# Keys turned by the vector engine from a second, split read, in a cross-attention, attention and expert kernel

## Reference

```
x (8,64,512), ctx (8,1601,512)
x = x + softmax((LN(x) Wq + bq)(ctx Wk + bk)^T / sqrt(512)) (ctx Wv + bv)   # cross-attention, 1 head
x = x + gated_attention(LN(x))    # 16 heads of 32; sigmoid((cos(q,k) - 0.295) * 15) with gates, then Wo
x = x + experts(LN(x))            # 8 experts, top 1, sigmoid of the best logit, SiLU-gated, 512 -> 256 -> 512
```

## Time and profile before

| | us |
|---|---|
| runs: median (lowest to highest) of 3 | 393.93 (393.82 to 394.73) |
| profiled execution: span, first to last instruction | 391.0 |
| TensorE busy in it | 363.3 |
| VectorE, ScalarE, GpSimd busy in it | 147.2, 93.3, 82.2 |
| bytes moved, mean rate | 56.48 MB, 144 GB/s |

### The profile page before, as it was taken

One profiled execution on the slowest core, in us unless ns is written; L12 is line 12 of the kernel. 1 busy time (PEld: TensorE's weight loads), 2 busy tenths in 40 slices (PEclk: granted clock), 3 DMA queues, 4 the chain that ended last, 5 costly groups with the idle time before them and its releaser, 6 DMA issues.

```text
span 391.0 us, 6077 instructions
## 1 busy us (share of the span) xinstructions
PE 363.3 (93%) x2346; PEld 232.2 (59%) x2346; DVE 147.2 (38%) x341; ACT 93.3 (24%) x191; POOL 82.2 (21%) x87
## 2 busy tenths in 40 slices
PE   1999999999999999999999999999889989799993
PEld 1786667435646544565654455653435869697781
DVE  4100365003616523351652444342362654155322
ACT  2222321213215331222541222241302400000000
POOL 4000243500215002022400201202322402511122
PEclk9999998999999999999999999999999999899998
DMA  7999200399700029710004950000693052920000
GB/s 256 409 404 351 93 0 2 107 341 373 309 2 0 2 80 382 264 27 0 0 0 174 380 200 0 2 0 2 230 421 157 3 214 71 324 104 18 29 24 25
DMA packets 13798, 56.48 MB, mean 144 GB/s; under 512 B 1574, under 2 KB 1606, under 8 KB 9680
## 3 DMA queue, kind: packets, MB, share of 16 engines
q1 hardware_dynamic: 11776, 50.35, 34.3%
q0 software_dynamic: 2000, 5.83, 4.2%
HBM read 53.03 MB, written 4.19 MB: 146 GB/s over the span
## 4 chain that ended last, share of the span: by engine, by line
PE 83%; DVE 6%; issue 3%; POOL 3%; ACT 2%; DMA 2%; DVEq 0%; ACTq 0%; POOLq 0%; SPq 0%
PE TR L911 14%; PE A L916 13%; PE ST L1005 12%; PE SC L982 12%; PE A L1191 8%; PE A L936 4%; PE A L958 4%; PE TR L916 4%; PE SC L1173 3%; PE A L911 2%; PE SC L1148 1%; DMA AW_sb<-rows,idxg_sb 1%; PE TR L992 1%; PE A L1123 1%; PE A L1053 1%
## 5 line engine op out<-in xcount | busy, mean ns | idle before, releaser
L260 DVE COPY CT_sb<-TR 128x512 f32<-128x512 f32 (+1 forms) x52 | 34.9, 672 | 64.5 <-PE TR L911 62.0
L911 PE MATMUL TR<-ident_sb,CTX_sb 128*128 128x128 f32 (+1 forms) x416 | 55.5, 274 | 3.4 <-ACT CT_sb L260 2.3
L911 PEld LDWEIGHTS TR<-ident_sb,CTX_sb 128*128 128x128 f32 (+1 forms) x416 | 44.5, 141 | 21.3 <-issue 13.9
L982 PE MATMUL SC<-CT_sb,qcur_sb 128*64 128x256 f32 x384 | 51.6, 391 | 0.0
L1005 PE MATMUL ST<-CTX_sb,PR_sb 128*64 128x512 f32 (+1 forms) x208 | 47.7, 599 | 0.9 <-ACT PR_sb L267 0.9
L260 ACT COPY CT_sb<-TR 128x512 f32<-128x512 f32 (+1 forms) x52 | 29.6, 569 | 63.4 <-PE TR L911 63.4
L982 PEld LDWEIGHTS SC<-CT_sb,qcur_sb 128*64 128x64 f32 x384 | 23.4, 136 | 14.5 <-issue 7.0
L1005 PEld LDWEIGHTS ST<-CTX_sb,PR_sb 128*64 128x64 f32 (+1 forms) x208 | 13.8, 136 | 24.4 <-issue 23.6
L916 PE MATMUL A<-AW_sb,normT_sb 128*128 128x512 f32 x48 | 22.0, 600 | 0.0
L399 POOL TENSOR_TENSOR rn_sb<-ss_sb,nhalf_sb 128x16 f32<-128x16 f32 x4 | 11.6, 2908 | 45.6 <-DVE ss_sb L709 45.6
L1148 PE MATMUL SC<-ident_sb 128*128 128x128 f32 x140 | 17.7, 278 | 0.0
(11 more groups left out here) (238 smaller groups left out, 488.0 us busy)
## 6 DMA issues: line engine op xcount, KB each, us to landing
CTX_sb<-ctx SPq DMA_DIRECT2D x24, 1024.0 KB, 8.2
CTX_sb<-wgu SPq DMA_DIRECT2D x4, 1024.0 KB, 9.4
CTX_sb<-wdn SPq DMA_DIRECT2D x5, 512.0 KB, 11.5
FF_sb<-wgu SPq DMA_DIRECT2D x2, 1024.0 KB, 14.1
rows<-XR_sb SPq DMA_DIRECT2D x3, 512.0 KB, 9.9
CTX_sb<-ctx SPq DMA_DIRECT2D x8, 130.0 KB
AW_sb<-x SPq DMA_DIRECT2D x2, 512.0 KB, 3.8
WQK_sb<-wq SPq DMA_DIRECT2D x1, 1024.0 KB, 8.2
```

Of the source, the lines that this page charges most:

```text
L260: copy(ctxT[:, grp % 2, k, :, (t % GT) * P:(t % GT) * P + w], turned_bank(TR[k])[:, :, 0:w]).then_inc(s[f"moved{k}"], 1)
L911: last = t_.transpose(bank[:, c * w:c * w + n], rows[:, c * P:(c + 1) * P], ident[0:n, 0:n])
L982: last = t_.matmul(out[q, :], qcur[:, c, q], ctxT[:, grp % 2, k, c, 0:n], start=(c == 0), stop=(c == DC - 1))
```

## The change

The transposes on TensorE (`turn_keys`, `moved`/`turned` handshakes) and the copies by ScalarE and VectorE are removed. Instead ctx is read from memory a second time, into the tile `split`, which lies in FF: for a group of 256 keys, both batches, 32 keys r lie on 32 partitions, 8 blocks b in the free direction, and each quad of 32 partitions holds another 128 of the 512 features. VectorE turns each batch of a group in one instruction in blocks of 32x32; features land interleaved, `4 p + c` on partition p, so wkT is read with a step of four in `bring`, and ctx rows are laid out by plain order (key `128 t + p`), in runs of 2 KB. `split` has three slots; four DMAs of 128 KB a group and queue are issued by SyncE (quads 0 and 1) and four by ScalarE (quads 2 and 3). A slot is refilled after its group is turned (`keysT_made`), and a group is turned two ahead of the scores. The first two experts go into FF after the last keys are turned.

```
+SP_QUADS, ACT_QUADS = (0, 1), (2, 3)
+SPLIT_AT = {0: 3, 1: 4, 4: 5, 6: 6}
+NEXT_AT = {9: 1, 11: 2, 13: 0}
-MOVES = KT + NCH // 2
+MOVES = NCH // 2
+        split = FF[:, 0:NSPLIT * 2 * GT * D].rearrange("p (s k b d) -> p s k b d", s=NSPLIT, k=2, d=P)
-        def move_keys(eng, copy, p, k, t):
...
+        def load_split(eng, quads, p, grp):
+            before_it = [(GROUPS - 1, 1), (4, 1), (5, 1)][grp] if grp < NSPLIT else (grp - NSPLIT, 0)
+            earlier(eng, "keysT_made", 2 * (GROUPS * (p - before_it[1]) + before_it[0] + 1))
+            slot, n = grp % NSPLIT, BLOCKS if grp < GROUPS - 1 else TAIL // Q
+            for quad in quads:
+                for k in range(2):
+                    src = A["ctx"][bass.ds(2 * p + k, 1), grp * GT * P:grp * GT * P + n * Q, quad * P:(quad + 1) * P]
+                    eng.dma_start(split[quad * Q:(quad + 1) * Q, slot, k, 0:n, :],
+                                 src.rearrange("a (b r) d -> r (a b) d", r=Q)).then_inc(s_split[slot], 16)
+            if grp == GROUPS - 1 and 0 in quads:
...
-                    src = A["ctx"][bass.ds(b, 1), 0:FULL * P, :].rearrange("a (p t) d -> p (a t) d", t=FULL)[:, lo:hi, :]
+                    src = A["ctx"][bass.ds(b, 1), lo * P:hi * P, :].rearrange("a (t p) d -> p (a t) d", p=P)
             load_x(0)
+            for grp in range(5):
+                load_split(sp, SP_QUADS, 0, grp)
             load_pair(0)
             load_weight(wv, "wv", "wv_in")
...
             load_weight(awv, "awv", "av_in")
+            load_split(sp, SP_QUADS, 0, 5)
+            load_split(sp, SP_QUADS, 0, 6)
+            for grp in range(NSPLIT):
+                load_split(sp, SP_QUADS, 1, grp)
             sp.wait_ge(s["qk_made"], 2 * DC)
             sp.wait_ge(s["c_made"], 1)
             load_weight(awo, "awo", "awo_in")
             load_pair(1)
+            def rest_of_pair(p):
+                load_split(sp, SP_QUADS, p, 3)
+                load_split(sp, SP_QUADS, p, 4)
+                load_x(p)
+                load_split(sp, SP_QUADS, p, 5)
+                load_split(sp, SP_QUADS, p, 6)
+            with sp.Fori(1, PAIRS - 1) as p:
+                rest_of_pair(p)
+                for grp in range(NSPLIT):
+                    load_split(sp, SP_QUADS, p + 1, grp)
+                load_pair(p + 1)
+                store_rows(p - 1)
+            rest_of_pair(PAIRS - 1)
+            sp.wait_ge(s["keysT_made"], 2 * GROUPS * PAIRS)
             for e in range(OWN):
                 load_expert(e)
...
+            for grp in range(NSPLIT):
+                load_split(act, ACT_QUADS, 0, grp)
             for half in range(2):
...
+                load_split(act, ACT_QUADS, 0, NSPLIT + half)
...
+            load_split(act, ACT_QUADS, 0, 5)
+            move_qk(False, 0)
+            move_qk(False, 1)
+            load_split(act, ACT_QUADS, 0, 6)
+            for grp in (1, 2, 0):
+                load_split(act, ACT_QUADS, 1, grp)
...
                 for u in range(2 * GROUPS):
+                    if u in SPLIT_AT:
+                        load_split(act, ACT_QUADS, p, SPLIT_AT[u])
+                    if u in NEXT_AT and not is_last(p):
+                        load_split(act, ACT_QUADS, p + 1, NEXT_AT[u])
...
+            def turn_keys(p, grp):
+                slot, n = grp % NSPLIT, BLOCKS if grp < GROUPS - 1 else TBLOCKS
+                dve.wait_ge(s_split[slot], SPLIT_DMAS[slot][-1] * p + SPLIT_DMAS[slot][grp // NSPLIT])
+                earlier(dve, "scored", GROUPS * p + (grp - 1 if grp else 0))
+                for k in range(2):
+                    v.transpose(ctxT[:, grp % 2, k, :, 0:n * Q].rearrange("p c (b r) -> p b c r", r=Q),
+                                split[:, slot, k, 0:n, :].rearrange("p b (r c) -> p b c r", c=DC)).then_inc(s["keysT_made"], 1)
...
                 for u in range(2 * GROUPS):
-                    move_keys(dve, v.tensor_copy, p, 1, GT + u)
+                    if u % 2:
+                        turn_keys(p, 2 + u // 2)
...
+                    if c >= 2 and not is_last(p):
+                        turn_keys(p + 1, c - 2)
...
-                    last = t_.matmul(AB[m % 2][:, n], wkT[:, c, m * P:(m + 1) * P], qpT[:, c, n], start=(c == 0), stop=(c == DC - 1))
+                    last = t_.matmul(AB[m % 2][:, n], wkT[:, c, m:D:DC], qpT[:, c, n], start=(c == 0), stop=(c == DC - 1))
...
-                        pe.wait_ge(s[f"moved{k}"], MOVES * p + min(lo + GT, KT))
+                    pe.wait_ge(s["keysT_made"], 2 * (GROUPS * p + grp + 1))
```

More of the change, by code:

```diff
@@ L16 @@
 GROUPS = -(-KT // GT)
+Q = 32
+QUADS = P // Q
+SP_QUADS, ACT_QUADS = (0, 1), (2, 3)
+BLOCKS = GT * P // Q
+TBLOCKS = -(-TAIL // Q)
+NSPLIT = 3
+SPLIT_DMAS = [[16 * n for n in (8, 16, 25)], [16 * n for n in (8, 16)], [16 * n for n in (8, 16)]]
 CHUNKS = [(0, 4), (4, 8), (8, FULL), (FULL, KT)]
@@ L227, in program @@
         s_ctx = [[sem(f"ctx_in{k}{c}") for c in range(NCH)] for k in range(2)]
+        s_split = [sem(f"split_in{i}") for i in range(NSPLIT)]
         s_w = [sem(f"expert_in{e}") for e in range(E)]
@@ L794, in _ @@
             dve.wait_ge(s["vec_in"], 16)
-            for t in range(GT):
-                move_keys(dve, v.tensor_copy, 0, 1, t)
+            turn_keys(0, 0)
+            turn_keys(0, 1)
             for u in range(2 * GROUPS):
@@ L810, in _ @@
                 move_numerators(dve, v.tensor_copy, 0, c)
+            turn_keys(1, 0)
+            turn_keys(1, 1)
             def pair(p, by_scores, by_max, by_sums):
-                for t in range(GT):
-                    move_keys(dve, v.tensor_copy, p, 1, t)
                 for u in range(2 * GROUPS):
@@ L938, in _ @@
                     last.then_inc(s["qp_made"], 1)
-            def turn_keys(p, t):
-                if t >= KT:
-                    return
-                w = P if t < FULL else TAIL
-                for k in range(2):
-                    for c, (lo, _) in enumerate(CHUNKS):
-                        if t == lo:
-                            pe.wait_ge(s_ctx[k][c], 16 * p + 16)
-                    earlier(pe, f"moved{k}", MOVES * p + t)
-                    turn_rows(TR[k], ctxb[0:w, k, t, :], w, P).then_inc(s[f"turned{k}"], 1)
             def bring(first, m):
@@ L997, in weigh @@
                 lo, hi = CHUNKS[c]
-                pe.wait_ge(s[f"moved{c % 2}"], MOVES * p + KT + c // 2 + 1)
+                pe.wait_ge(s[f"moved{c % 2}"], MOVES * p + c // 2 + 1)
                 if c == 0:
                     pe.wait_ge(s["exp_made"], NCH * (p + 1))
+                for k in range(2):
+                    pe.wait_ge(s_ctx[k][c], 16 * p + 16)
                 for t in range(lo, hi):
@@ L1091, in scores @@
             def scores(p, by_scores):
-                first = isinstance(p, int) and p == 0
-                if not first:
-                    turn_keys(p, 0)
-                turn_keys(p, 1)
-                if first:
+                if isinstance(p, int) and p == 0:
                     bring(False, 0)
```

34 lines of the change are left out of this document (9 added, 25 removed).

## The result

The changed kernel takes **439.52 us** (median of 4 runs, 436.36 to 442.06), the kernel before 393.88 on the same chip: a ratio of 1.117, 95% interval 1.111 to 1.122. It is 45.6 us slower, where I forecast 18.3 slower; the time lies 1.5 us above my range. The execution profiled spans 437.4 us, 46.4 more than before.

What follows compares the result with a forecast made beforehand. TensorE was taken as the bound only while transfers stay ahead. Pair 0 +16.6, clock +1, pairs 1 to 3 +0.1, +1.5 and -0.9 made +18.3 on 393.9: 412 us, range 388 to 438.

Steps and rivals of the forecast that it cites:

- What bounds the kernel; transfers have nothing to spare at two places: TensorE bounds only while transfers stay ahead; DMA engines are full the first 40 us and about 20 us around pair borders.
- The turn's price, 1.22 us: VectorE's transpose of 128x1024, priced from a reduction and copies: 1.22 us each, 2.44 us a group.
- the 16-byte step as a rival: VectorE's turn slowed by reading its source with a 16-byte step: 2.3 us a turn, 430 us in all; chance 0.12.
- The packet's price, 37.5 ns: Split loads' 512-byte packets, taken midway between 31 and 44 ns: 37.5 ns, 218 GB/s, 4.8 us a group.
- The narrow-writes rival: Split loads into few partitions set the rate, 44 ns or more a packet: 420 to 428 us; chance 0.12.
- Pair 0, +17.6: First pair: group 5 lands at 72.0 us and TensorE stands still about 20 us; 16.6 us, plus 1 us for the clock.
- The wait at "a2", from group 3's landing: Pair 2: group 3 lands at 172.0; "norm" stands behind its turn, so "a2" starts at 175.1 instead of 170.5, 4.6 us late.
- Both signs that were to show the forecast wrong: In the profile after: group 5 landing before 60 us, or "a2" not waiting for DMA.
- After a2 six tiles are gone, 5.8 us. Given back: Later pairs behind "a2": TensorE saves 5.8 us of transposes, some given back; net 3.1 us, leaving pair 2 at +1.5.
- Weight loads with the step: TensorE's loads of wkT with a step of four: taken as 0, hidden under 384-column matmuls; 3.2 us if they doubled.
- ScalarE's four issues ahead of its work for "y": Pairs 1 to 3: ScalarE issues four DMAs before it moves "on", 1.8 us; y starts at 159.8 instead of 160.9.
- The faster rival: Small packets go at the rate of bytes, 19.2 ns, deciding below 24 ns: 387 us; chance 0.15.

Runs made afterwards that it cites:

- e1_dense: Changed kernel with VectorE's turn reading adjacent source elements instead of a 16-byte step, wkT's columns laid out to match by the host; 428.55 us, ratio 1.086.
- p2: Changed kernel with split loads in 512-byte runs, each DMA writing all 128 partitions, two DMAs a group instead of eight, keys mixed up; 429.7 us.
- the fills: Changed kernel with small matmuls put where TensorE waits, in two runs with different counts and places; 440.5 and 438.2 us.
- c5_need: Changed kernel with step-free turn, norm before group 3's turn, SyncE's queue by need (pair 0: awq, awk, chunk 1 before groups 5, 6); 385.69 us, ratio 0.978.
- the three orders: Changed kernel with one edit each: later pairs' groups 3, 4 before ctx chunks; pair 0's groups 5, 6 earlier; norm before turn 3; 429.6, 432.9, 423.0 us.
- c3: As c5_need, but with awq, awk and ctx chunk 1 behind groups 5 and 6 in pair 0's SyncE queue; 398.8 us.
- t2_fill_all: Changed kernel with filling matmuls: 66 ahead of group 5 in pair 0, in the middle pairs 14 ahead of "on" and 22 ahead of a2; 438.2 us.

## Why the prediction was wrong, point by point

- **What bounds the kernel; transfers have nothing to spare at two places**: right. Both new waits stand exactly there.
- **The turn's price, 1.22 us: wrong, 1.99.** It was right for the instruction with adjacent elements (1222 and 557 ns in e1_dense). I had the 16-byte step as a rival at 0.12 and let the nearest rows decide, although none of them reads with a step. e1_dense shows it: 11.0 of the 27.3 us missed. That the forecast met 1222 ns so closely is partly luck, since it was put together from a reduction and a copy, of which neither turns anything.
- **The packet's price, 37.5 ns**: within the ends, 43.6 alone and 33.9 with both halves under way; the wide 27.6 and the narrow 43.6 are close to my 31 and 44. Group 5 landed at 77.4, 5.4 us after my 72.0. The narrow-writes rival was right for the stretches in which SyncE's half went alone; p2 against the changed kernel, one run with fewer issues, puts the width at about 10 us. The 2 KB packets cost what I had (775 in 4 us in the stretch from 50 to 54 us, 388 GB/s).
- **Pair 0, +17.6: the mechanism right, the size 23.4.** The landing came 5.4 us late, and the bias 8.5 us behind it instead of 7.1, since the turns are slow (6.7 in e1_dense).
- **The wait at "a2", from group 3's landing: right in place and time.** Landed at 206.1 in pair 2, which is 171.4 on the clock of before (less the 34.7 us by which the pair began late), forecast 172.0; "a2" 5.3 us late, forecast 4.6. Both signs that were to show the forecast wrong, a landing before 60 us and an "a2" that does not wait for a transfer, stayed away: the mechanism of the waits was right, their price and what follows them was not.
- **"After a2 six tiles are gone, 5.8 us. Given back": this is the step that failed in the later pairs.** I took TensorE's time behind a wait as before, less the tiles, and gave the clock no term there; I had sized it once, at 1 us, for pair 0. From "a2" to the sums my sum had 31.9 us in pair 2, and 38.8 were measured. In place of the forecast the matmuls behind the waits ran at a granted clock of 0.52 and 0.53, 5.5 us more, and align0 waited 3.9 us for a long turn, where I had 1.4. That it is not the turn's price alone, e1_dense shows: with a turn of 1.22 us, as forecast, "a2" is 4.2 us late, and from there to the sums it still takes 36.6 us; pairs 1 to 3 cost 6.3, 5.8 and 1.5 us, where I had 0.1, 1.5 and -0.9. That a good part is the clock, the fills show: 2.3 to 2.9 us came back behind "a2" where they held it. How the rest divides between the clock behind align0 and the waits themselves was not separated.
- **Weight loads with the step**: 322 for 203 ns, hidden beside the 384-column matmuls (552 ns each for 548, and the 16 behind the scores 7.10 us as before), as I took; the 128-column ones, ahead of the first scores, took 399 for 276 ns, which pair 0's wait covers.
- **ScalarE's four issues ahead of its work for "y"**: priced 1.8 us, they took 2.95 in pair 2.
- **Ending and rounds +0**: right, 0.3.
- **The faster rival** (24 ns or less) fell: no stretch of 512-byte packets that was read came below 27.6 ns.

How much of the waits belongs to the change itself stays partly open: c5_need keeps the split loads and the turns on VectorE and beats the kernel before, so removing the step, the queue order and the place of one turn is enough to make 7.9 us of gain out of 45.6 us of loss. Split reads into 128 partitions in c5's order, with right results and all engines at work, were not tried. Which of the three orders contained in c3 and c5 gives how much in pairs 1 to 3 was not tried one by one, nor was the 8 KB form of the ctx chunks beside split loads.

## What to carry to other kernels

When work is moved from a full engine to one that waits for transfers, read the order of the receiving engine's program: a turn that waits for a landing must not stand ahead of a short step that the full engine needs. Queue transfers in the order in which they are needed and in which their buffers come free, and look in the trace for gaps of the DMA engines as well as for full stretches. Price an instruction by a row with the same access pattern, or take the dear end when no row has it. Where a wait is forecast, give the matmuls behind it a term for the lower clock.

## What the runs showed of the hardware

- A transpose of 32x32 blocks on VectorE of 128x1024 fp32: 1222 ns with adjacent source elements, 1993 with a step of 16 bytes; of 128x384: 557 and 853 ns.
- Stationary loads of 128x128 fp32: 203 to 214 ns adjacent, 322 with a step of four elements.
- 512-byte packets: 176 GB/s into 32-partition pieces of one half, 248 with both halves, 290 into 128 partitions. A transfer whose outermost dimension is 4 moved 83 GB/s with two queues under way.
- The 32 matmuls of one column: 3.66 us in the kernel before at a granted clock of 1.00; in t2_fill_all 6.99 us at 0.50 (1.2 GHz), though TensorE had been busy for 15.0 us at 1.00 until 2.2 us before group 5's scores.
